# A GNN layer on one core: the second group's slot transposes move from TensorE to VectorE and memory, and its distances, gathers and next messages move behind conv2

## What is computed

```
h = jnp.maximum(_layernorm(x, axis=-1), 0.0)
c = relu(bn(conv1d(h, conv1_w, 0)));  c = bn(conv1d(c, conv2_w, 8))      # 17 taps
x_conv = relu(c + h)
s = h @ w_se.T + b_se                                                     # 3 numbers a node
dist = sq[:, :, None] + sq[:, None, :] - 2.0 * einsum('bnd,bmd->bnm', s, s)
A = exp(-dist) * adj;   msg = relu(h @ w_msg.T + b_msg);   x_nmp = A @ msg
gi = [x_conv, x_nmp] @ w_ih.T + b_ih;   gh = h @ w_hh.T + b_hh
r, z = sigmoid(gi_r + gh_r), sigmoid(gi_z + gh_z);  n = tanh(gi_n + r * gh_n)
out = x + (1 - z) * n + z * h
```

## Time and profile before

| | us |
|---|---|
| median of the runs (lowest, highest) | 280.0 (279.77, 280.37) |
| the profiled execution | 280.33 |
| its span, first to last instruction | 278.5 |
| TensorE busy, matmul | 271.4 (97%) |
| TensorE busy, weight loads | 245.9 (88%) |
| VectorE busy | 243.7 (87%) |
| ACT busy | 163.4 (59%) |
| POOL busy | 65.3 (23%) |
| chain that ended last: share of TensorE | 93% |

### The profile page before, as it was taken

One profiled execution on the slowest core, in us unless ns is written; L12 is line 12 of the kernel. 1 busy time (PEld: TensorE's weight loads), 2 busy tenths in 40 slices (PEclk: granted clock), 3 DMA queues, 4 the chain that ended last, 5 costly groups with the idle time before them and its releaser, 6 DMA issues.

```text
span 278.5 us, 5224 instructions
## 1 busy us (share of the span) xinstructions
PE 271.4 (97%) x1800; PEld 245.9 (88%) x1800; DVE 243.7 (87%) x550; ACT 163.4 (59%) x275; POOL 65.3 (23%) x127
## 2 busy tenths in 40 slices
PE   7999999999999999999999999999999999999993
PEld 6699978999889988899889998899889998899883
DVE  6899999898999889987999989987999887984666
ACT  3787469737753677517754567527674276541563
POOL 7900022720234002610216002530016100340000
PEclk9999999999999999999999999999999999999999
DMA  7950413654244545173532635363440604053002
GB/s 238 353 64 0 160 69 151 227 63 166 79 152 61 139 155 183 45 100 100 225 154 43 117 119 171 132 94 107 151 153 10 108 11 151 2 62 60 2 0 75
DMA packets 20797, 31.00 MB, mean 111 GB/s; under 512 B 9778, under 2 KB 14644, under 8 KB 19892
## 3 DMA queue, kind: packets, MB, share of 16 engines
q1 hardware_dynamic: 17552, 26.47, 28.4%
q0 software_dynamic: 3072, 4.20, 11.3%
q10 hardware_dynamic: 148, 0.01, 0.0%
HBM read 25.64 MB, written 8.70 MB: 123 GB/s over the span
## 4 chain that ended last, share of the span: by engine, by line
PE 93%; DMA 2%; DVE 2%; ACT 2%; issue 1%; DVEq 0%; ACTq 0%
PE ps L1348 24%; PE ps L1350 24%; PE ps L1349 24%; PE ps L1416 5%; PE ps L1459 5%; PE ps L1641 3%; DMA aff<-x_nm 2%; PE ps L1491 2%; PE ps L1482 2%; PE ps L1488 2%; PE ps L1437 1%; PE ps L1368 1%; ACT cp L559 1%; PE ps L1427 0%; DVE gn L1144 0%
## 5 line engine op out<-in xcount | busy, mean ns | idle before, releaser
L1348 PE MATMUL ps<-v_hi,wt_hi 128*128 128x256 f32 x280 | 78.8, 281 | 0.0
L1350 PE MATMUL ps<-v_hi,wt_lo 128*128 128x256 f32 x280 | 78.8, 281 | 0.0
L1349 PE MATMUL ps<-v_lo,wt_hi 128*128 128x256 f32 x280 | 78.6, 281 | 0.0
L1348 PEld LDWEIGHTS ps<-v_hi,wt_hi 128*128 128x128 f32 x280 | 52.7, 188 | 0.9 <-ACT msg L614 0.4
L1349 PEld LDWEIGHTS ps<-v_lo,wt_hi 128*128 128x128 f32 x280 | 52.7, 188 | 0.5
L1350 PEld LDWEIGHTS ps<-v_hi,wt_lo 128*128 128x128 f32 x280 | 52.6, 188 | 0.0
L427 POOL TENSOR_TENSOR scale<-vpe,neg_half 128x8 f32<-128x8 f32 x6 | 10.6, 1758 | 83.2 <-DVE scale L868 83.2
L596 ACT ACTIVATE mbs<-ps,par 128x256 f32<-128x256 f32 x24 | 12.1, 502 | 29.8 <-DVE y L998 17.6
L1348 PE MATMUL ps<-h_hi,wt_hi 128*128 128x512 f32 (+1 forms) x65 | 25.8, 398 | 0.5 <-ACT gate L692 0.4
L1350 PE MATMUL ps<-h_hi,wt_lo 128*128 128x512 f32 (+1 forms) x65 | 25.0, 384 | 0.0
L1349 PE MATMUL ps<-h_lo,wt_hi 128*128 128x512 f32 (+1 forms) x65 | 24.9, 384 | 0.0
(11 more groups left out here) (186 smaller groups left out, 640.1 us busy)
## 6 DMA issues: line engine op xcount, KB each, us to landing
w<-ln_rows SPq DMA_DIRECT2D x6, 1024.0 KB, 4.8
mask<-adj_t SPq DMA_DIRECT2D x8, 512.0 KB, 3.3
out<-x_t SPq DMA_DIRECT2D x7, 512.0 KB, 5.3
out<-gate POOLq DMA_DIRECT2D x14, 256.0 KB, 4.1
xt<-x_t SPq DMA_DIRECT2D x6, 512.0 KB, 3.6
xin<-x_nm SPq DMA_DIRECT2D x5, 512.0 KB, 5.2
slot_rows<-turned SPq DMA_DIRECT2D x24, 32.0 KB, 3.1
rows<-slot_rows SPq DMA_DIRECT2D x6, 128.0 KB, 2.5
```

The costliest lines, as they stand in the source:

```text
L1348: pe.matmul(dst, wt_hi[:, blk, :], hi, start=start, stop=False)
L1349: pe.matmul(dst, wt_hi[:, blk, :], lo, start=False, stop=False)
L1350: return pe.matmul(dst, wt_lo[:, blk, :], hi, start=False, stop=stop)
```

## The change

`BY_TRANSPOSE` becomes 0, so that group 1 goes by VectorE and memory. Its slots are filled by ACT and VectorE, as group 0's are (`slots_first` and `slots_low_first` get the group as an argument), POOL no longer does `distances(1)`, and VectorE does `turn(1)` between the parts of `v_low_u(1, ...)`. On TensorE group 1 has no transposes; behind the nine sub-convolutions come h's gates, the distances, conv1 of group 2, xc's part of gates r and z (`xc_ahead`, new), both gathers, the messages of group 2, xc's part of gate n (`xc_candidate`, new), n's part and h's gates for half 1. ACT's and VectorE's lists for group 1 follow that, and on ACT `update_rows(0, 0)` moves ahead of all four tiles of `ln_rows_first(1, ...)`. Groups 2 to 7 keep their lists.

```diff
-        BY_TRANSPOSE = 1
+        BY_TRANSPOSE = 0
@@ def distances(engine, g):
-            if g <= BY_TRANSPOSE + 1:
-                upto(engine, rows_ps, g)
-            else:
-                engine.wait_ge(turned_ready, g - 1 - BY_TRANSPOSE)
+            engine.wait_ge(turned_ready, g - 1 - BY_TRANSPOSE)
@@ POOL's loop
-                distances(pool, g)
+                if g > 1:
+                    distances(pool, g)
@@ ACT, messages(g)
-                if g == 0:
-                    slots_first(0)
+                if g <= 1:
+                    slots_first(g, 0)
@@ ACT's list
             reset_rows(0, 0)
-            ln_rows_first(1, (4, 5))
             update_rows(0, 0)
-            ln_rows_first(1, (6, 7))
+            ln_rows_first(1, range(4, GB))
...
             messages(1)
+            slots_first(1, 1)
             v_high_u(1, 0)
+            slots_first(1, 2)
             v_high_u(1, 1)
@@ ACT's loop, what g = 1 does now
+                m_shared(g, 1)
+                    h_high(g + 1, 0)
+                    h_high(g + 1, 1)
+                    graphs_of(g + 1, 0)
+                    graphs_of(g + 1, 1)
+                m_shared(g, 2)
+                xc_high(g)
+                ghn_rows(g, 0)
+                if g == 1:
+                    exponent(g)
+                    conv1_rows(g + 1, 0, 0)
+                    conv1_rows(g + 1, 1, 1)
+                    v_high_b(g + 1, 0)
+                    n_high(g, 0, 5)
+                    n_high(g, 1, 7)
+                    v_high_b(g + 1, 1)
@@ VectorE's list
             v_low_b(1, 0)
             v_low_b(1, 1)
+            slots_low_first(1, 0)
             level2_u(1)
-            for part in range(3):
-                v_low_u(1, part)
+            slots_low_first(1, 1)
+            v_low_u(1, 0)
+            v_low_u(1, 1)
+            turn(1)
+            v_low_u(1, 2)
@@ VectorE's loop
-                if g <= BY_TRANSPOSE:
-                    masked(g, 0)
-                    masked(g, 1)
...
                 xc_low(g, 0)
                 xc_low(g, 1)
-                if g > BY_TRANSPOSE:
+                if g == 1:
+                    masked(g, 0)
+                    masked(g, 1)
+                else:
                     n_low(g, 0, 5)
                     n_low(g, 1, 7)
...
                     level2_b(g + 1, 1)
-                    level1(g + 1)
-                    v_low_b(g + 1, 0)
+                    if g == 1:
+                        n_low(g, 0, 5)
+                        v_low_b(g + 1, 0)
+                        n_low(g, 1, 7)
+                        raw_messages(g + 1)
+                        level1(g + 1)
@@ TensorE
+            def xc_ahead(g):
+                xc = (xc_hi[:, cols(0)], xc_lo[:, cols(0)])
+                pe.wait_ge(xc_lo_ready, NCH * g + 1)
+                three(bank(4), IH(R, 0), *xc, False, False)
+                three(bank(6), IH(Z, 0), *xc, False, False)
+
+            def xc_candidate(g):
+
+                pe.wait_ge(n_lo_ready, NCH * g + 1)
+                three(bank(5), IH(N, 0), xc_hi[:, cols(0)], xc_lo[:, cols(0)], True, False)
@@ TensorE's loop
                 gates_h(g, 0, ahead)
...
+                if g == 1:
+
+                    distance(g)
+                    conv1(g + 1, 0, 0)
+                    conv1(g + 1, 1, 1)
+                    xc_ahead(g)
                     gather(g, 0, 5)
                     gather(g, 1, 7)
+                    messages(g + 1)
+                    xc_candidate(g)
                     gates_n(g, 0)
+                    gates_h(g, 1, ahead)
```

More of the change, by code:

```diff
@@ L278, in distances @@
             s = s_sb[:, :, 0:3]
-            base = 10 * (g - 1)
+            base = 10 * (g - 2)
             engine.tensor_copy(six(left, 0), twice(s)).then_inc(s_steps, 1)
@@ L619, in raw_messages, with slots_first @@
                 act.activation(msg[:, 0:8, :], msg[:, 0:8, :], ACT.Relu).then_inc(msg_ready, 2)
-            def slots_first(step):
+            def slots_first(g, step):
                 left, right = slots[:, 0], slots[:, 1]
@@ L627, in slots_first @@
                 if step == 0:
-                    act.wait_ge(s_ready, 2)
+                    act.wait_ge(s_ready, 2 * g + 2)
                     act.wait_ge(pool_set, 5)
+                    upto(act, rows_ps, g)
                     act.activation(hi, s_sb[:, :, 0:3].unsqueeze(2).broadcast_to([P, GB, 2, 3]),
@@ L752, in _ @@
             messages(0, 3)
-            slots_first(1)
+            slots_first(0, 1)
             m_shared(0, 1)
-            slots_first(2)
+            slots_first(0, 2)
             lot_high(11)
@@ L791, in _ @@
                     m_shared(g, 0)
-                if g <= BY_TRANSPOSE:
-                    factor_rows(g)
-                    exponent(g)
[L795 to L810, removed]
+                m_shared(g, 1)
+                if ahead:
+                    h_high(g + 1, 0)
[3 more added lines that the diff above has]
+                m_shared(g, 2)
+                if g > 1:
+                    exponent(g)
+                xc_high(g)
+                ghn_rows(g, 0)
+                if g == 1:
                     exponent(g)
-                if g > BY_TRANSPOSE:
-                    xc_high(g)
-                    ghn_rows(g, 0)
+                    conv1_rows(g + 1, 0, 0)
+                    conv1_rows(g + 1, 1, 1)
+                    v_high_b(g + 1, 0)
                     n_high(g, 0, 5)
                     n_high(g, 1, 7)
+                    v_high_b(g + 1, 1)
                 else:
[L818 to L824, removed]
+                    n_high(g, 0, 5)
+                    n_high(g, 1, 7)
+                    if ahead:
+                        conv1_rows(g + 1, 0, 0)
+                        conv1_rows(g + 1, 1, 1)
+                        v_high_b(g + 1, 0)
+                        v_high_b(g + 1, 1)
                 if ahead:
@@ L1082, in slots_low_first @@
                 if step == 0:
-                    dve.wait_ge(s_ready, 2)
+                    dve.wait_ge(s_ready, 2 * g + 2)
                     dve.scalar_tensor_tensor(out=ssq[:], in0=s, scalar=-0.5, in1=s, op0=ALU.mult,
                                              op1=ALU.mult).then_inc(slot_sq, 1)
-                    dve.wait_ge(slot_hi, 1)
+                    dve.wait_ge(slot_hi, 2 * g + 1)
                     dve.tensor_tensor(left[:, :, 6:12].rearrange("p b (r k) -> p b r k", k=3),
@@ L1206, in _ @@
             join_b(0, 1)
-            slots_low_first(0)
+            slots_low_first(0, 0)
             v_low_u(0, 2)
-            slots_low_first(1)
+            slots_low_first(0, 1)
             lot_low(8)
@@ L1281, in _ @@
                 join_y(g, 0, 1)
-                if g <= BY_TRANSPOSE:
-                    n_low(g, 0, 5)
                 if ahead:
                     h_low(g + 1, 0)
[L1286 to L1300, removed]
+                    h_low(g + 1, 1)
+                add_shared(g, 1)
+                join_y(g, 1, 0)
+                join_y(g, 1, 1)
+                if g > 1:
                     masked(g, 0)
                     masked(g, 1)
-                    if g + 2 < NG:
-                        ln_stats(g + 2)
+                if g + 2 < NG:
+                    ln_stats(g + 2)
                 xc_low(g, 0)
                 xc_low(g, 1)
-                if g > BY_TRANSPOSE:
+                if g == 1:
+                    masked(g, 0)
+                    masked(g, 1)
+                else:
                     n_low(g, 0, 5)
@@ L1314, in _ @@
                     level2_b(g + 1, 1)
-                    level1(g + 1)
-                    v_low_b(g + 1, 0)
+                    if g == 1:
[4 more added lines that the diff above has]
+                        level1(g + 1)
+                    else:
+                        level1(g + 1)
+                        v_low_b(g + 1, 0)
                     v_low_b(g + 1, 1)
-                if ahead:
                     reset(g, 0)
@@ L1321, in _ @@
                     update(g, 0)
-                    raw_messages(g + 1)
+                    if g > 1:
+                        raw_messages(g + 1)
                     for part in range(3):
@@ L1702, in _ @@
                 gates_h(g, 0, ahead)
-                if g > BY_TRANSPOSE:
+                if g == 1:
[3 more added lines that the diff above has]
+                    xc_ahead(g)
                     gather(g, 0, 5)
                     gather(g, 1, 7)
[L1706 to L1709, removed]
+                    messages(g + 1)
+                    xc_candidate(g)
                     gates_n(g, 0)
-                    gates_xc(g, 0)
+                    gates_h(g, 1, ahead)
                 else:
+                    gather(g, 0, 5)
+                    gather(g, 1, 7)
+                    if ahead:
+                        conv1(g + 1, 0, 0)
+                        conv1(g + 1, 1, 1)
                     gates_xc(g, 0)
                     gates_n(g, 0)
```

(5 more changed lines are left out.)

17 lines of the change are left out of this document (8 added, 9 removed).

## The result

The changed kernel takes 282.42 us (281.75 to 282.67, 4 runs) beside 280.12 for the kernel before: a ratio of 1.0074, with a 95% interval of 1.0054 to 1.0095. A second set of executions (`e11_changed_again`, 281.47 to 281.85, 6 runs) has a median of 281.72 beside 279.86, 1.0053 (1.0033 to 1.0073). The differences of the medians are 2.3 and 1.9 us, the ratios make it 2.1 and 1.5, and both intervals lie above 1. So the change makes the kernel slower, by 1.5 to 2.3 us; the forecast was +1.9, at 281.9. One execution of e12, 685.85 us where its others take some 282, was a slow one and is left out.

A forecast was written before the change was run, and what follows sets the result against it. TensorE was taken to bound the kernel, busy nearly throughout, with VectorE close behind. Terms -0.44 - 0.12 - 0.08 + 0.29 + 0.48 + 0.30 + 1.37 + 0.13 = +1.93, said +1.9, on the median 280.0 gave 281.9 us; range 280.2 to 283.0.

The forecast's parts named there:

- What bounds it: Whole kernel: TensorE is busy nearly throughout, matmuls plus few waits; VectorE, within a tenth of it, is to be watched.
- Work that leaves TensorE: Group 1 on TensorE: transposes -0.44, distances -0.12, one block of gathers and messages -0.08; together -0.64 us.
- ACT's order in group 0: update_rows(0, 0) moved earlier: TensorE about 0.70 us earlier, then idle for h_low(1, 0); booked 0, bounds -0.70 to 0.
- Messages: Group 1's message rows on ACT come after a slot copy, so TensorE enters conv2 later, uncovered: +0.29 us.
- VectorE up to the joins: Group 1: TensorE waits for the two join_y before sub-convolutions 7 and 8: +0.48 and +0.30 us.
- ACT and VectorE up to xc: Group 1: TensorE reaches xc's matmuls before xc_low(1, 0) is ready and waits; largest term, +1.37 us.
- three waits: Group 1 on TensorE: for the first join_y +0.48, the second +0.30, and xc_low +1.37 us.
- Behind it: After xc: no further wait in group 1; the wait at group 2's distances grows, +0.13 us, between -0.20 and +0.60.
- the 10.9 us of the earlier trace: Group 2's time from the start of turn to its distances, used for the slots' way through memory.
- The sign that group 1 takes 34.6: Evidence named beforehand that the forecast is right: group 1 takes 34.6 us, groups from 3 on 32.2 as before.
- TensorE's saved work comes out: Rival: VectorE and ACT have enough slack, only the message delay stands; -0.55 us, 279.4, chance 0.12.

The follow-up runs named there:

- e11_changed_again: The changed kernel itself, unaltered, run again with more executions: 281.72 us, 1.0053 of the kernel before.
- e12: Changed kernel with ln_apply(2, 1) moved behind join_y(1, 0, 1) on VectorE, run again beside the changed kernel on one chip: 282.29 us, 1.0078 of the kernel before.
- e3: Kernel before, with only update_rows(0, 0) moved ahead of all four tiles of ln_rows_first(1, ...) on ACT: 280.14 us, ratio 1.001.
- e2: Changed kernel with the scaling and output of update(0, 1) moved behind h_low(2, 1) on VectorE: 280.19 us, 1.0012 of the kernel before.
- e8: Changed kernel with m_shared(1, 2) moved on ACT from behind both graphs_of(2, ...) to between the two h_high(2, ...): 280.33 us, 1.0000 of the kernel before.
- e5: Changed kernel with ln_apply(2, 1) moved behind join_y(1, 0, 1) in VectorE's list of group 1, first run: 282.33 us.
- e4: Kernel before, with one more ACT copy into an unused tile between the copy of s and group 1's message rows: 280.17 us, ratio 1.0007.
- e10: Changed kernel with m_shared(1, 2) earlier on ACT, update(0, 1)'s end later on VectorE, group 1's slot copies behind message rows: 279.84 us, 0.9983 of kernel before.

## Why the prediction was right

**What bounds it.** Right: VectorE was the engine to watch, and the first two joins and `xc_low` are where TensorE waits.

**Work that leaves TensorE, -0.64.** Measured -0.52: group 1 without its waits is 34.33 - 2.00 - 0.11 of restart = 32.22, before it was 32.85 - 0.11 = 32.74. The transposes and distances are worth what the rows said, but one block of gathers and messages saves nothing of the 0.08 I gave it. The messages follow the gathers without a pause, and both together take 3.51 and 0.08 for the change behind them; apart they took 1.78 and 1.80. The first of the messages comes 0.08 late there: the 16 gathers take 1.78 to 1.79 up to it, and 1.70 in group 2 up to the gate behind them:

```profile
72.80 1.95 PE L1453 MATMUL ps<-aff,msg 128*128 128x128 f32 x16
...
76.31 0.48 PE L1342 MATMUL ps<-xc_hi,wt_hi 128*128 128x512 f32 x1
```

**ACT's order in group 0, 0.** Right, and e3 shows it alone.

**Messages, +0.29.** The slot copy and the message rows stand 0.14 apart, 0.15 in group 0; the two pieces of message rows were a little faster (ends 51.07, not 51.11), the entry is 0.26 later:

```profile
49.66 0.17 ACT L605 ACTIVATE s_sb<-ps 128x8 f32<-128x8 f32 x1
49.87 0.24 ACT L630 ACTIVATE slots<-s_sb 128x48 fp32r<-128x48 f32 x1
50.01 0.80 ACT L610 ACTIVATE msg<-ps 128x768 f32<-128x768 f32 x1
50.70 0.37 ACT L612 ACTIVATE msg<-ps 128x256 f32<-128x256 f32 x1
```

**VectorE up to the joins, +0.48 and +0.30.** Less the 0.36 of start-up, the first `join_y` started at 62.33 - 0.36 = 61.97 where 62.08 was forecast (before: 62.92); the waits were 0.37 and 0.29.

**ACT and VectorE up to xc, +1.37.** 1.34. The three rows that carry it, again 0.36 late by start-up; the first has the idle time that e2 and e8 used:

```profile
67.42 0.69 DVE L1004 TENSOR_TENSOR y<-y,mbs 128x512 f32<-128x512 f32 x1 [1.68 <-ACT mbs L594]
...
69.02 1.64 DVE L846 BATCH_NORM_STATS2 stats<-xin 128x6 f32<-128x128 f32 x8
70.57 1.28 DVE L1019 SCALAR_TENSOR_TENSOR xc_lo<-y,xc_hi 128x512 fp32r<-128x512 f32 x2
```

What the prediction put loosely: it listed three waits as three terms. Their sum is right only because each arrival was counted from the release before it. As costs they are one, the release of xc against TensorE's undisturbed arrival; e5 and e12 show that (while xc's wait stands; e8 shows what they cost without it), and e2 that moving the whole chain by 1.52 gains 1.53 and not 2.0.

**Behind it, +0.13.** Wrong in sign against that trace (-0.12; +0.05 against e3 and e4), within its bounds: there is no wait at group 2's distances now. `turn(2)` started 2.28 us after the group (2.24 forecast), so that part held, but from turn to distances 10.57 us were enough:

```profile
87.74 0.43 DVE L1071 STREAM_TRANSPOSE turned<-slots 128x256 f32<-128x256 f32 x1
```

```profile
98.31 0.62 PE L1431 MATMUL ps<-right_rows,rows 128*128 128x512 f32 x2
```

The step that failed is the 10.9 us of the earlier trace rows, taken from one execution in which SP needed 3.32 us to issue four loads (2.48 here). e3 and e4, whose group 2 is that of the kernel before, take 32.19 and 32.22, not 32.38: the 0.20 of waiting there is not the kernel's own. e5's execution has such a wait again, at 10.82 from turn to distances. In group 1 the way through memory was hidden, as forecast.

**The number.** Forecast +1.93, in the trace +1.62, or +1.8 against e3 and e4. The work that leaves was put 0.12 too large, the three waits together 0.15 too large (2.15, and 2.00 measured), group 2 some 0.1 to 0.25. The first error works against the others, so that 281.9 lies so near to 281.72 is in part luck. The sign that group 1 takes 34.6 doesn't follow from them, 32.85 - 0.64 + 2.15 = 34.36, and 34.33 was measured.

The rivals: "TensorE's saved work comes out" needed VectorE 1.4 us earlier. e10 comes nearest: of the 0.52 of work saved, 0.36 goes in xc's wait, and group 1 is 0.16 shorter than before. By the Trainium skill ("Perfetto Trace Analysis", "Identifying the Most-Contended Engine") the engine with the highest occupancy is to be optimized first, here TensorE with 97% in matmuls. Its weight loads, which the page wants read for TensorE's headroom, have 88% and VectorE 87%. In this kernel relieving TensorE by 0.5 us gave a loss, until the engines that feed it were ordered for an earlier TensorE. The rule on 128x128 transposes of the Trainium skill ("VectorE: DVE Perf Modes", "Rules for kernel authors") would have left them on TensorE, where the four cost 0.44. The measured sign agrees, but the loss came from order and not from the transposes' new place: with them there e8 is level with the kernel before by its times.

No run moves the transposes alone, or keeps them on TensorE with the new order of gathers and messages. So what the way through memory is worth by itself is not shown beyond the 0.56 of transposes and distances in the rows.

## What to carry to other kernels

When work is taken from the engine that bounds a kernel, every wait behind it comes due earlier by that much; follow the last release of the stretch backwards through the other engines, and count its arrival against the bounding engine's, before booking a gain. Do not add the waits on the way as costs of their own. Where a chain is late, look first for a short eviction or copy that is ready but queued behind long work that nobody waits for yet (here 0.5 us behind two copies, 2.3 together), and check that a step moved out of the way does not fill the slack of the next wait.

## What the hardware showed

Float32 gathers and messages run at 0.10 to 0.11 us a matmul whether they stand in blocks of 8, 16 or 32 (0.81, 1.70 and 3.51 us). A change from them back to the split matmuls costs about 0.08 once (0.31 to the next start where 0.234 is natural, 0.20 where 0.118 is), and merging gathers with messages gained nothing. The nine DMAs of group 2's slots took 10.8 us from the start of the turn to the last landing in the kernel before and 10.2 in the changed one, with the same code for them.
